# Norms, transposes and stores of a decoder layer's cross stage, one tile at a time

## The chip, the cores and the metric

The kernel runs on one core of a Trainium2 chip. The core has TensorE (PE, with its weight loads PEld), VectorE (DVE), ScalarE (ACT), GpSimd (POOL) and SyncE (SP, which issues the DMAs here). The metric is the device time in microseconds of one execution, median over runs. All data is f32; matmuls in f32r run in one pass and those in f32 in several.

## The reference, cut to what matters

One layer over 8 batches of 512 tokens with 512 features and 16 heads of 32: a causal self-attention with a second linear attention ("memory"), then cross-attention to a context, then two experts with a top-2 gate. Behind each stands a layer norm of the sum with its input.

```python
x = _layernorm(x + _L0_attn_ref(x, ...))
x = _layernorm(x + _L0_xattn_ref(ctx, ctx, x, Wv, Wk, Wq, Wo, bo))   # second norm
x = _layernorm(x + _L0_ffn_ref(x, gate_w, w0, b0, w1, b1))           # third norm

# _L0_xattn_ref: softmax(q k / sqrt(512)) v over 16 heads, then
out @ Wo.T + bo
# _L0_ffn_ref
weights = softmax(tokens @ gate_w); topk_w, topk_idx = top_k(weights, 2)
e0 = silu(x @ w0.T + b0); e1 = silu(x @ w1.T + b1)
out = e0 * fw[:, 0:1] * (fidx[:, 0:1] == 0) + e1 * fw[:, 1:2] * (fidx[:, 1:2] == 1)
```

## The kernel before, in words

Three stages follow each other: self, memory, cross. The change is in the cross stage, which starts in the last rounds of the memory stage. A batch has 4 **tiles** of 128 tokens and 4 **groups** of 4 heads. The stage is written as a line of **slots** n = 0 to 639. Sixteen slots (`SLOTS`) make a group, 64 (`BATCH_SLOTS`) a batch, and `NS` = 512 slots hold all scores. Each engine runs a function of its own over the same slots (`cross_slot_tensor`, `_scalar`, `_vector`, `_gpsimd`, `_sync`) and executes its instructions strictly in that order. Semaphores alone tie the engines. Which slot an instruction stands in is thus its place in its engine's queue. `at` is the slot within the group.

In each slot PE makes one transposed score product (L1353, `bank 2 + n % 2`) and, 22 slots ahead (`CROSS_LEAD`), one product for row maxima (L1325). ACT turns the first into an exp (L1572), DVE takes the maximum of the second (L1335). PE's product of slot n waits for the exp of slot n - 2. Every fourth slot PE multiplies exps and values (L1385). POOL adds the exps of a group in three additions of 128 x 2048 (L1795, at slots 7, 11 and 15 of the group), and PE sums them over partitions at slot 4 of the next group (L1418, "totals"). DVE makes four reciprocals of them (L1643) and y (L1650). At `at` 11 PE transposes the next group's maxima, at 12 ACT copies them (L1547), at 13 DVE subtracts for the low part (L1655) and SP stores both as two rows into the operand stack (`store_shift`, "cross_shift"). The first score product of the next group waits for these.

Batch b's **work behind** its attention runs in the slots of the following batches (`behind(n)` gives the batch and its own slot number, 0 to 127; batch b's slot 0 is n = 64 (b + 1)). All four tiles go through each step together. The output projection and bias are at slots 12 to 27 (L1452, L1432, PE), with the residual addition L1670 and the statistics L138, L140 on DVE tile by tile. POOL computes the factors of all four tiles with four small operations of 128 x 4 at slot 29 (`Norm.factors`, L146 to L152). ACT applies the second norm at slots 31 to 34 (L157). PE transposes at 35 to 38, one chunk of features across all tiles each (L1464), ACT copies the high part x2t_hi (L1587), DVE makes the low part x2t_lo (L1677). The gate is at 39 to 42: 12 matmuls with 8 weight columns and 512 tokens (L163 to L165), whose result is copied and transposed back at 44 (L1592, L1477). DVE picks the top two from 128 x 32 (`cross_gate_first`, `cross_gate_weights`, 15 small operations). The eight units of experts (4 tiles x 2 experts) are at slots 48 to 71 (L1503). Each goes through ACT's tanh (L1601), DVE's silu (L1687), ACT's weighting (L1606) and POOL's addition to x2 (L1775). The third norm has its statistics at 62, 68, 74 and 80, factors of all tiles at 81, applies at 83 to 86, and one store of 1 MB at 87 (L1848).

Batch 7's work has no scores beside it. It runs in slots 512 to 639 by the same functions.

## Time and profile before

| | us |
|---|---|
| median of 3 runs | 1872.0 |
| lowest and highest | 1866.68, 1873.97 |
| profiled execution | 1871.82 |
| its span | 1869.9 |

| engine | busy us | share of the span |
|---|---|---|
| PE | 1743.1 | 93% |
| DVE | 1266.4 | 68% |
| POOL | 1084.1 | 58% |
| ACT | 967.5 | 52% |

The profile is one execution. A line is named by its number in the kernel; a name such as `bank` or `x` is a tile without its buffer number, and a helper's line is shared by all its callers (L157 is every norm's apply). Idle time is put down to what came last before the engine went on.
### The profile page before, as it was taken

The page shows a single profiled execution, that of the slowest core. Times are in us where ns is not written, and L with a number is a line of the kernel's source. Part 1 is how long each engine was busy: PE and PEld are TensorE (multiplying, and loading weights), DVE is VectorE, ACT ScalarE, POOL GpSimd, SP SyncE. Part 2 cuts the span into 40 slices and gives each one's busy share as a digit, 9 for nine tenths or more (in the row PEclk, how much of TensorE's full clock was granted, in tenths as well). Part 3 has the DMA queues.
Part 4 walks back from the last instruction along what each step waited for, and adds up shares of the span by engine and source line. Part 5 has one row for each costly group of instructions (what it writes and reads, how often), then busy time and mean ns, then how long its engine had stood idle before and what let it go on. Part 6 is the DMA issues. An engine that isn't in the chain of part 4 may idle for free.

```text
span 1869.9 us, 29831 instructions
## 1 busy us (share of the span) xinstructions
PE 1743.1 (93%) x10442; PEld 1092.0 (58%) x10442; DVE 1266.4 (68%) x2747; ACT 967.5 (52%) x1893; POOL 1084.1 (58%) x741
## 2 busy tenths in 40 slices
PE   5999999999999889999977999999999999999886
PEld 4666666666666368877733465554645546455444
DVE  5677777777777477778766667667677677676532
ACT  3555555555555423433455555555555555555533
POOL 2555565656554646544577675575665766666552
PEclk9999999999999789999989999999999999999998
DMA  6465655555554545666356334334433344333100
GB/s 195 136 159 152 158 154 151 162 142 166 140 154 123 173 143 164 205 199 192 101 143 145 94 94 119 93 89 119 106 99 97 92 113 119 103 96 102 35 23 23
DMA packets 166496, 237.21 MB, mean 127 GB/s; under 512 B 21318, under 2 KB 72518, under 8 KB 166348
## 3 DMA queue, kind: packets, MB, share of 16 engines
q1 hardware_dynamic: 166348, 235.31, 45.6%
q8 instruction: 84, 1.38, 0.3%
q14 instruction: 64, 0.52, 0.1%
HBM read 91.57 MB, written 41.94 MB: 71 GB/s over the span
## 4 chain that ended last, share of the span: by engine, by line
PE 73%; DVE 7%; POOL 5%; ACT 4%; DMA 4%; issue 3%; SPq 2%; ACTq 0%; POOLq 0%; DVEq 0%
PE bank L1503 9%; PE bank L163 8%; PE bank L164 6%; PE bank L165 6%; PE bank L1452 5%; PE bank L1385 5%; PE bank L313 4%; PE bank L1353 4%; PE bank L258 4%; PE bank L1325 4%; POOL cross_added L1795 4%; PE bank L300 4%; DVE bank L1643 2%; PE bank L278 2%; DVE cross_negmax L1335 2%
## 5 line engine op out<-in xcount | busy, mean ns | idle before, releaser
L1335 DVE TENSOR_REDUCE cross_negmax<-bank 128x1 f32<-128x512 f32 x512 | 342.4, 678 | 213.7 <-PE bank L1325 209.6
L1572 ACT ACTIVATE cpt<-bank 128x512 f32<-128x512 f32 x512 | 299.8, 594 | 216.0 <-PE bank L1353 212.6
L487 DVE CUSTOM_DVE_ANT_0 bank<-bank,future 128x128 f32<-128x128 f32 (+3 forms) x512 | 246.7, 488 | 172.9 <-PE bank L300 172.2
L372 ACT ACTIVATE pt<-bank 128x256 f32<-128x256 f32 (+3 forms) x512 | 224.2, 441 | 256.8 <-PE bank L258 256.0
L1795 POOL TENSOR_TENSOR cross_added<-cross_added,cpt 128x2048 f32<-128x2048 f32 x64 | 292.3, 4566 | 58.1 <-ACT cpt L1572 57.9
L1325 PE MATMUL bank<-cqk 96*128 96x512 f32 x512 | 262.2, 516 | 22.6 <-DMA cqk<-cstage 12.3
L1795 POOL TENSOR_TENSOR cross_added<-cpt,cpt 128x2048 f32<-128x2048 f32 x32 | 146.5, 4577 | 184.9 <-ACT cpt L1572 184.9
L1353 PE MATMUL bank<-cqk 98*128 98x512 f32 x512 | 228.3, 447 | 26.0 <-ACT cpt L1572 18.4
L551 POOL TENSOR_SCALAR_AFFINE_SELECT pt<-pt 128x512 f32<-128x512 f32 x128 | 81.3, 635 | 251.7 <-ACT pt L372 251.6
L163 PE MATMUL bank<-xt_hi,w_hi 128*128 128x512 f32 x384 | 168.9, 440 | 18.8 <-DVE w_lo L445 15.7
L258 PE MATMUL bank<-qk 98*128 98x256 f32 (+2 forms) x512 | 180.1, 355 | 4.2 <-DMA qk<-self_shift 2.5
L1353 PEld LDWEIGHTS bank<-cqk 98*128 98x128 f32 x512 | 98.4, 192 | 146.0 <-ACT cpt L1572 68.1
L300 PE MATMUL bank<-qk 96*128 96x256 f32 (+2 forms) x512 | 165.8, 328 | 4.1 <-DMA qk<-stage 4.1
L164 PE MATMUL bank<-xt_hi,w_lo 128*128 128x512 f32 x384 | 153.5, 400 | 0.0
L165 PE MATMUL bank<-xt_lo,w_hi 128*128 128x512 f32 x384 | 152.3, 397 | 0.0
L1643 DVE RECIPROCAL bank<-bank 128x128 f32<-128x128 f32 x128 | 121.9, 955 | 41.4 <-PE bank L1418 41.4
L1325 PEld LDWEIGHTS bank<-cqk 96*128 96x128 f32 x512 | 99.2, 195 | 79.0 <-DVE cross_negmax L1335 34.0
L1385 PE MATMUL bank<-cpt,cv 128*32 128x512 f32 x1024 | 140.6, 622 | 0.0
L258 PEld LDWEIGHTS bank<-qk 98*128 98x128 f32 x512 | 98.0, 193 | 69.7 <-ACT pt L372 45.1
L1452 PE MATMUL bank<-wo,cy 128*128 128x512 f32 x256 | 134.4, 614 | 0.0
L1775 POOL TENSOR_TENSOR x<-x,tanh 128x512 f32<-128x512 f32 x64 | 82.5, 1289 | 85.4 <-ACT tanh L1606 84.3
L500 DVE RECIPROCAL bank<-bank 128x128 f32<-128x128 f32 x128 | 122.1, 958 | 8.8 <-PE bank L278 8.8
(172 smaller groups left out, 3463.5 us busy)
## 6 DMA issues: line engine op xcount, KB each, us to landing
qk<-stage SPq DMA_DIRECT2D x384, 128.0 KB, 2.3
cqk<-cstage SPq DMA_DIRECT2D x384, 128.0 KB, 2.3
scratch_memory<-memory SPq DMA_DIRECT2D x32, 512.0 KB, 3.8
ma<-scratch_memory SPq DMA_DIRECT2D x32, 512.0 KB, 4.0
raw<-in_x_t SPq DMA_DIRECT2D x32, 256.0 KB, 2.8
v<-in_x SPq DMA_DIRECT2D x32, 256.0 KB, 3.3
scratch_y_ar<-y_ar SPq DMA_DIRECT2D x32, 256.0 KB, 2.2
my_ar<-scratch_y_ar SPq DMA_DIRECT2D x32, 256.0 KB, 4.5
```

The source lines that it names most:

```text
L163: pe.matmul(out, a[0], b[0], start=first, stop=False)
L164: pe.matmul(out, a[1], b[0], start=False, stop=False)
L165: return pe.matmul(out, a[0], b[1], start=False, stop=last)
L258: pe.matmul(bank[:, 0:SEQ - q0], kq[0:98, 1, j, first:first + P], kq[0:98, 0, j, q0:SEQ], start=True, stop=True).then_inc(s.pe_st, 1)
L300: pe.matmul(bank[:, 0:max(keys, 256)], kq[0:96, 0, j, tile_of(qt)], kq[0:96, 1, j, 0:max(keys, 256)], start=True, stop=True).then_inc(s.pe ...
L487: dve.tensor_tensor_reduce(out=scores, in0=scores, in1=sh.future[:, SEQ - P * (qt + 1):SEQ], scale=-1.0, scalar=-NEG, op0=ALU.add, op1=ALU ...
L1325: pe.matmul(max_bank(sh, m)[:, :], kq[0:96, 0, jm, tile_of(qt)], kq[0:96, 1, jm, :], start=True, stop=True).then_inc(s.pe_mx, 1)
L1335: dve.reduce_max(s.negmax[gm % 2][:, col:col + 1], max_bank(sh, m)[:, :], AX, negate=True).then_inc(s.dve_max, 1)
L1353: pe.matmul(sh.bank[2 + n % 2][:, :], kq[0:98, 1, j, tile_of(kt)], kq[0:98, 0, j, :], start=True, stop=True).then_inc(s.pe_st, 1)
L1385: done = pe.matmul(sh.bank[4][rows_of(j), :], s.v[g % 2][:, kt, rows_of(j)], s.pt[step % 3][:, j, :], start=(kt == 0), stop=(kt == TILES - ...
L1572: act.activation(s.pt[step % 3][:, j, :], sh.bank[2 + n % 2][:, :], ACT.Exp, scale=SCALE_CROSS).then_inc(s.act_exp, 1)
L1795: pool.tensor_tensor(s.added[:, :, :], old[:, :, :], s.pt[step % 3][:, :, :], ALU.add).then_inc(s.pool_add, 1)
```

## The change

Both norms of the cross stage get a class of their own, `TileNorm`, which has the statistics, factors and apply of one tile and counts semaphores per tile. In the batches 0 to 6 the second norm's factors stand at slots 18, 22, 26, 30 and its applies at 20, 24, 28, 32. The transposes are by tile (one tile's four chunks of features), at 25, 29, 31, 34, with the copies of the high and low part in the next two slots. The gate and its transposition back stand one slot earlier. The third norm's factors stand at 63, 69, 75, 81, its applies at 65, 71, 77, 83, and each tile has its own store of 256 KB at 66, 72, 78, 84, with two semaphores in turn. The shift rows' subtraction and stores move from `at` 13 to 12, on DVE and on SP.

Batch 7 leaves the slots. These end at 536, and a written-out part follows on each engine (`tail_...`). There three quarters of the projection of tiles 0 and 1 come ahead of the wait for the last group's y. Each tile then has norm, transposes, gate, two experts, third norm and store behind one another; the gate multiplies with the tokens as weights (128 x 128) and the 8 gate columns as data, so that the logits need no transposition. x3, in place of x2, lies in the operand stack that the last groups no longer use.

```diff
+class TileNorm:
+    def __init__(self, nc, sb, sem, name):
+        self.stats, self.mv = sb(f"{name}_stats", [P, TILES, 6]), sb(f"{name}_mv", [P, TILES, 2])
+        self.rstd, self.shift = sb(f"{name}_rstd", [P, TILES]), sb(f"{name}_shift", [P, TILES])
+        self.power = sb(f"{name}_power", [P, TILES])
+        self.vec, self.root, self.applied = sem(f"{name}_vec"), sem(f"{name}_root"), sem(f"{name}_applied")
+    def statistics(self, dve, b, k, r):
+        t = TILES * b + k
+        if b > 0:
+            dve.wait_ge(self.root, 4 * (t - TILES) + 5)
+        dve.bn_stats(self.stats[:, k, :], r).then_inc(self.vec, 1)
+        dve.wait_ge(self.vec, 2 * t + 1)
+        dve.bn_aggr(self.mv[:, k, :], self.stats[:, k, :]).then_inc(self.vec, 1)
+    def factors(self, pool, b, k):
+        t, ks = TILES * b + k, slice(k, k + 1)
+        pool.wait_ge(self.vec, 2 * t + 2)
+        if b > 0:
+            pool.wait_ge(self.applied, t - TILES + 1)
+        pool.tensor_scalar(self.rstd[:, ks], self.mv[:, ks, 1], EPS, None, ALU.add).then_inc(self.root, 1)
+        pool.wait_ge(self.root, 4 * t + 2)
+        pool.tensor_tensor(self.rstd[:, ks], self.rstd[:, ks], self.power[:, ks], ALU.pow).then_inc(self.root, 1)
+        pool.wait_ge(self.root, 4 * t + 3)
+        pool.tensor_tensor(self.shift[:, ks], self.mv[:, ks, 0], self.rstd[:, ks], ALU.mult).then_inc(self.root, 1)
+        pool.wait_ge(self.root, 4 * t + 4)
+        pool.tensor_scalar(self.shift[:, ks], self.shift[:, ks], -1.0, None, ALU.mult).then_inc(self.root, 1)
+    def apply(self, act, b, k, out, r):
+        act.wait_ge(self.root, 4 * (TILES * b + k) + 5)
...
-CROSS_SLOTS = range(SLOTS_BEHIND[LAST + 7][1], NS + 2 * BATCH_SLOTS)
+CROSS_SLOTS = range(SLOTS_BEHIND[LAST + 7][1], NS + 25)
...
+        self.x3 = Place(nc, ATTENTION + LAST_FREE * STACK_BYTES, TOP)("x3", [P, TILES, DIM])
...
+LAST_BATCH = BATCH - 1
 def behind(n):
     b, r = divmod(n, BATCH_SLOTS)
-    return [(bb, r + more) for bb, more in ((b - 1, 0), (b - 2, BATCH_SLOTS)) if 0 <= bb < BATCH]
-PROJECT, APPLY, TRANSPOSE, GATE, LOGITS, EXPERT = 12, 31, 35, 39, 44, 48
-STATS3, FACTORS3, APPLY3, STORE = 62, 81, 83, 87
+    return [(bb, r + more) for bb, more in ((b - 1, 0), (b - 2, BATCH_SLOTS)) if 0 <= bb < LAST_BATCH]
+PROJECT, FACTORS, APPLY, TRANSPOSE = 12, (18, 22, 26, 30), (20, 24, 28, 32), (25, 29, 31, 34)
+GATE, LOGITS, EXPERT = 38, 43, 48
+STATS3, FACTORS3, APPLY3, STORE = (62, 68, 74, 80), (63, 69, 75, 81), (65, 71, 77, 83), (66, 72, 78, 84)
...
+    if slot in TRANSPOSE:
+        k = TRANSPOSE.index(slot)
+        pe.wait_ge(s.ln2.applied, TILES * b + k + 1)
+        if k < 2:
+            pe.wait_ge(s.dve_po, TILES * b + 3 + k)
         else:
-            pe.wait_ge(s.dve_x2t, GROUPS * b + c - 1)
-        for k in range(TILES):
-            done = pe.transpose(sh.bank[6 + c % 2][:, tile_of(k)], s.x2[:, k, tile_of(c)], sh.ident[:, :])
+            pe.wait_ge(s.dve_x2t, TILES * b + k - 1)
+        for c in range(GROUPS):
+            done = pe.transpose(sh.bank[6 + k % 2][:, tile_of(c)], s.x2[:, k, tile_of(c)], sh.ident[:, :])
...
+        pe.wait_ge(s.dve_x2t, TILES * (b + 1))
...
+    if slot in APPLY:
+        k = APPLY.index(slot)
+        if b >= 1:
+            act.wait_ge(s.out_stored[k % 2], 16 * (2 * b - 1 + k // 2))
+        s.ln2.apply(act, b, k, s.x2[:, k, :], s.x1[:, k, :])
+    if slot - 1 in TRANSPOSE:
+        k = TRANSPOSE.index(slot - 1)
         if k == 0 and b >= 1:
-            act.wait_ge(s.out_stored, 16 * b)
-        s.ln2.apply(act, b, k, s.x2[:, k, :], s.x1[:, k, :])
-    if TRANSPOSE + 1 <= slot < TRANSPOSE + 1 + GROUPS:
-        c = slot - TRANSPOSE - 1
-        if c == 0 and b >= 1:
             act.wait_ge(s.pe_ex, UNITS * b)
-        act.wait_ge(s.pe_x2t, GROUPS * b + c + 1)
-        act.activation(s.x2t_hi[:, c, :], sh.bank[6 + c % 2][:, :], ACT.Copy).then_inc(s.act_x2t, 1)
+        x2t_high(act, s, sh.bank[6 + k % 2], b, k)
...
+    if slot in APPLY3:
+        k = APPLY3.index(slot)
...
-    if at == 13 and 0 <= g + 1 < NG:
+    if at == 12 and 0 <= g + 1 < NG:
...
+    if slot - 2 in TRANSPOSE:
+        k = TRANSPOSE.index(slot - 2)
+        x2t_low(dve, s, sh.bank[6 + k % 2], b, k)
...
+    if slot in STATS3:
+        k = STATS3.index(slot)
...
+        if slot in FACTORS:
+            s.ln2.factors(pool, b, FACTORS.index(slot))
...
+        if slot in FACTORS3:
+            s.ln3.factors(pool, b, FACTORS3.index(slot))
...
+def cross_store(sp, s, b, k, x):
+    sp.wait_ge(s.ln3.applied, TILES * b + k + 1)
+    if 2 * b + k // 2 > 0:
+        sp.wait_ge(s.out_stored[k % 2], 16 * (2 * b + k // 2))
+    sp.dma_start(s.t["out"][b, tile_of(k), :], x[:, k, :]).then_inc(s.out_stored[k % 2], 16)
...
-    if at == 13 and 0 <= g + 1 < NG:
+    if at == 12 and 0 <= g + 1 < NG:
...
+        if slot in STORE:
+            cross_store(sp, s, b, STORE.index(slot), s.x2)
...
+def tail_tensor(pe, s, cw, sh):
+    pe.wait_ge(s.act_exp, NS)
+    pe.wait_ge(s.dve_max, NS)
+    for k in (0, 1):
+        tail_project(pe, s, cw, sh, k, range(GROUPS - 1))
+    for k in (0, 1):
+        tail_project(pe, s, cw, sh, k, (GROUPS - 1,))
+    tail_project(pe, s, cw, sh, 2, range(GROUPS))
+    tail_transposed(pe, s, sh, 0)
+    tail_project(pe, s, cw, sh, 3, range(GROUPS))
+    tail_transposed(pe, s, sh, 1)
+    for k in range(TILES):
+        tail_gate(pe, s, cw, sh, k)
+        for i in range(2):
+            tail_expert(pe, s, cw, sh, 2 * k + i)
+        if k + 2 < TILES:
+            tail_transposed(pe, s, sh, k + 2)
...
+def tail_project(pe, s, cw, sh, k, chunks):
+    b = LAST_BATCH
+    for c in chunks:
+        if c == 0:
+            cross_bias(pe, cw, sh.bank[k], 0)
+        pe.wait_ge(s.dve_norm, (TILES + 1) * (GROUPS * b + c + 1))
+        done = pe.matmul(sh.bank[k][:, :], s.y[:, (GROUPS * b + c) % (GROUPS + 1), tile_of(k)], cw.wo[:, c, :],
+                         start=False, stop=(c == GROUPS - 1))
+        if c == GROUPS - 1:
+            done.then_inc(s.pe_po, 1)
...
+def tail_gate(pe, s, cw, sh, k):
+    pe.wait_ge(s.dve_x2t, GROUPS * LAST_BATCH + k + 1)
+    pe.wait_ge(s.dve_po, TILES * LAST_BATCH + k + 1)
+    for c in range(GROUPS):
+        done = triple(pe, sh.bank[k][:, 0:EXPERTS], (s.x2t_hi[:, c, tile_of(k)], s.x2t_lo[:, c, tile_of(k)]),
+                      (cw.gate_hi[:, c, :], cw.gate_lo[:, c, :]), c == 0, c == GROUPS - 1)
+    done.then_inc(s.pe_gate, 1)
...
+def tail_scalar(act, s, sh):
+    b = LAST_BATCH
+    act.wait_ge(s.pe_st, NS)
+    act.wait_ge(s.pe_mx, NS)
+    for k in range(TILES):
+        s.ln2.apply(act, b, k, s.x3[:, k, :], s.x1[:, k, :])
+        if k in (1, 2):
+            if k == 1:
+                act.wait_ge(s.pe_ex, UNITS * LAST_BATCH)
+            x2t_high(act, s, sh.bank[4 + (k - 1) % 2], b, k - 1)
+    for k in range(TILES):
+        act.wait_ge(s.dve_gate, GATE_OPS * (b + k) + GATE_FIRST)
+        act.activation(gate_scratch(sh.bank[k], 1, 1), s.ge[:, k:k + 1, :], ACT.Exp).then_inc(s.act_gate, 1)
+        tail_tanh(act, s, sh, 2 * k)
+        tail_weigh(act, s, 2 * k)
+        tail_tanh(act, s, sh, 2 * k + 1)
+        if k + 2 < TILES:
+            x2t_high(act, s, sh.bank[4 + k % 2], b, k + 2)
+        if k >= 1:
+            s.ln3.apply(act, b, k - 1, s.x3[:, k - 1, :], s.x3[:, k - 1, :])
+        tail_weigh(act, s, 2 * k + 1)
+    s.ln3.apply(act, b, TILES - 1, s.x3[:, TILES - 1, :], s.x3[:, TILES - 1, :])
...
+def x2t_high(act, s, bank, b, k):
+    act.wait_ge(s.pe_x2t, TILES * b + k + 1)
+    act.activation(s.x2t_hi[:, :, tile_of(k)], bank[:, :].rearrange("p (c q) -> p c q", q=P),
+                   ACT.Copy).then_inc(s.act_x2t, 1)
...
+def tail_vector(dve, s, sh):
+    b = LAST_BATCH
+    dve.wait_ge(s.x1_landed, 16 * (b + 1))
+    for k in range(TILES):
+        dve.wait_ge(s.pe_po, TILES * b + k + 1)
+        dve.tensor_tensor(s.x1[:, k, :], sh.bank[k][:, :], s.x1[:, k, :], ALU.add).then_inc(s.dve_po, 1)
+        dve.wait_ge(s.dve_po, TILES * b + k + 1)
+        s.ln2.statistics(dve, b, k, s.x1[:, k, :])
+        if k >= 2:
+            x2t_low(dve, s, sh.bank[4 + k % 2], b, k - 2)
+    for k in range(TILES):
+        dve.wait_ge(s.pe_gate, b + k + 1)
+        cross_gate_first(dve, s, sh.bank[k], b + k, k, 1)
+        cross_gate_weights(dve, s, sh.bank[k], b + k, UNITS * b, k, 1)
+        tail_silu(dve, s, sh, 2 * k)
+        if k >= 1:
+            tail_statistics(dve, s, k - 1)
+        tail_silu(dve, s, sh, 2 * k + 1)
+        if k + 2 < TILES:
+            x2t_low(dve, s, sh.bank[4 + k % 2], b, k + 2)
+    tail_statistics(dve, s, TILES - 1)
...
+def x2t_low(dve, s, bank, b, k):
+    dve.wait_ge(s.act_x2t, TILES * b + k + 1)
+    dve.tensor_tensor(s.x2t_lo[:, :, tile_of(k)], bank[:, :].rearrange("p (c q) -> p c q", q=P),
+                      s.x2t_hi[:, :, tile_of(k)].bitcast(F32), ALU.subtract).then_inc(s.dve_x2t, 1)
...
+def tail_gpsimd(pool, s):
+    b = LAST_BATCH
+    for k in range(TILES):
+        s.ln2.factors(pool, b, k)
+    for u in range(UNITS):
+        x = s.x3[:, u // 2, :]
+        pool.wait_ge(s.act_w, UNITS * b + u + 1)
+        pool.wait_ge(s.pe_x2t, GROUPS * b + u // 2 + 1)
+        if u % 2 == 1:
+            pool.wait_ge(s.pool_x2, UNITS * b + u)
+        pool.tensor_tensor(x, x, s.tanh[u % 2][:, :], ALU.add).then_inc(s.pool_x2, 1)
+        if u >= 2 and u % 2 == 0:
+            s.ln3.factors(pool, b, u // 2 - 1)
+    s.ln3.factors(pool, b, TILES - 1)
```

## Rows read from the trace of the kernel before

**Rows 1.** Windows of two batches: span, busy us (count) PE PEld DVE ACT POOL, clock, DMA

```profile
1173.50:1286.90 113.40, 108.15 (x488) 60.55 (x488) 78.40 (x140) 63.68 (x114) 73.15 (x33) 0.97 0.40 103
1286.90:1398.90 112.00, 106.73 (x488) 59.01 (x488) 78.34 (x140) 63.46 (x114) 73.18 (x33) 0.98 0.40 104
```

**Rows 2.** Waits of PE, 905 to 1800 us: engine line <- releaser: total, times, longest

```profile
PE bank L1353 <- ACT cpt L1572: 18.4, 27, 2.6
...
PE bank L1353 <- DMA cqk<-cross_shift: 7.3, 15, 1.0
PE bank L163 <- DVE x2t_lo L1677: 6.5, 7, 0.9
```

**Rows 3.** Timeline, PE, 1286 to 1312: start, us, operation xcount [idle before <-releaser]

```profile
1286.91 0.50 PE L1353 MATMUL bank<-cqk 98*128 98x512 f32 x1 [0.63 <-DMA cqk<-cross_shift]
...
1289.91 0.50 PE L1353 MATMUL bank<-cqk 98*128 98x512 f32 x1 [0.22 <-ACT cpt L1572]
...
1291.10 0.50 PE L1353 MATMUL bank<-cqk 98*128 98x512 f32 x1 [0.46 <-ACT cpt L1572]
...
1292.77 0.50 PE L1353 MATMUL bank<-cqk 98*128 98x512 f32 x1 [0.95 <-ACT cpt L1572]
...
1296.08 1.04 PE L1418 MATMUL bank<-cross_added,ones 128*32 128x512 f32 x8
...
1298.79 0.66 PE L1464 MATMUL bank<-ident,x 128*128 128x128 f32 x4 [0.33 <-DVE x2t_lo L1677]
...
1300.84 0.39 PE L163 MATMUL bank<-x2t_hi,gate_hi 128*8 128x512 f32 x1 [0.92 <-DVE x2t_lo L1677]
...
1311.68 0.51 PE L1353 MATMUL bank<-cqk 98*128 98x512 f32 x1 [0.31 <-DMA cqk<-cross_shift]
```

**Rows 4.** Timeline, ACT, 1288 to 1289 us

```profile
1288.56 0.81 ACT L157 ACTIVATE x<-cx,ln_shift,ln_rstd 128x512 f32<-128x512 f32 x1 [2.54 <-POOL ln_shift L152]
```

**Rows 5.** Timeline, POOL, 1281 to 1295 us

```profile
1281.85 4.59 POOL L1795 TENSOR_TENSOR cross_added<-cross_added,cpt 128x2048 f32<-128x2048 f32 x1 [2.16 <-ACT cpt L1572]
...
1286.83 1.04 POOL L148 TENSOR_TENSOR ln_rstd<-ln_rstd,ln_power 128x4 f32<-128x4 f32 x1
1287.95 0.20 POOL L150 TENSOR_TENSOR ln_shift<-ln_mv,ln_rstd 128x4 f32<-128x4 f32 x1
...
1288.43 1.26 POOL L1757 TENSOR_TENSOR cstage<-cstage 128x512 fp32r<-128x512 f32 x1
1289.93 4.56 POOL L1795 TENSOR_TENSOR cross_added<-cross_added,cpt 128x2048 f32<-128x2048 f32 x1 [0.23 <-ACT cpt L1572]
```

**Rows 6.** Timeline, PE, 1250 us

```profile
1250.68 0.50 PE L1325 MATMUL bank<-cqk 96*128 96x512 f32 x1 [1.05 <-DVE cross_negmax L1335]
```

**Rows 7.** Windows of 3 us behind stalls: columns as in rows 1

```profile
1180.00:1183.00 3.00, 2.92 (x11) 2.44 (x11) 1.29 (x2) 2.19 (x5) 1.08 (x1) 0.50 0.83 191
1252.00:1255.00 3.00, 3.00 (x9) 1.07 (x11) 0.97 (x3) 1.12 (x2) 2.86 (x3) 0.53 0.02 5
```

**Rows 8.** Timeline, PE, at the last batch's first projection

```profile
1800.24 0.47 PE L1432 MATMUL bank<-bias_rows,bias_ones 128*128 128x512 f32 x1 [1.30 <-DVE cy L1650]
```

**Rows 9.** Chain of waits, 1799 to 1870 us: start, us, engine tile line xcount

```profile
1811.71 3.45 PE bank L1452 x8
...
1818.94 2.94 ACT x L157 x4
...
1821.92 1.13 PE bank L1464 x4
...
1850.15 2.80 PE bank L1503 x12
...
1862.42 0.81 ACT x L157
```

**Rows 10.** DMA issues: out<-in engine op xcount, KB each, us to landing

```profile
x_group<-scratch_x SPq DMA_DIRECT2D x32, 256.0 KB, 2.9
```

**Rows 11.** Groups by line, 905 to 1800: xcount | busy, mean ns | idle

```profile
L1702 DVE TENSOR_REDUCE gate_max<-bank 128x4 f32<-128x32 f32 x7 | 1.2, 169 | 0.0
```

166 lines of the change are left out of this document (96 added, 70 removed).

## The prediction

> **What bounds the kernel now.** I read the stretches first. From 1173 to 1737 us the cross stage repeats itself, one batch of 64 slots in 113.4 or 112.0 us, with PE busy 107 to 108 of it, DVE 78, POOL 73, ACT 63 [rows 1]. So PE sets the pace, the others have room on average, and only what makes PE wait, or adds to its work, can move this stage. The waits of PE come next: by releaser they are ACT's exps (18.4 us), the DMA of the shift rows (7.3) and x2t_lo (6.5) [rows 2]. PE's timeline places them, alike in each of batches 0 to 6. In one batch, slots 32 to 48, they are 0.63 (shift rows, slot 32), 0.22, 0.46 and 0.95 (exps, slots 33 to 35), 0.33 (transpose) and 0.92 (gate) for x2t_lo, and 0.31 (shift rows, slot 48): together 3.82 us [rows 3]. The exps are late because ACT, which works in order, stands 2.54 us before the first of four applies of the second norm, for POOL's factors of all four tiles; POOL makes these at slot 29, behind a 4.6 us addition [rows 4, 5]. A stall of 1.05 us near slot 75 is DVE's: reciprocals, silu and norm statistics stand together there [rows 6]. TensorE's granted clock fell to its lower level of 1.2 GHz (0.53) behind that stall, and in the batch of 113.4 us also behind the exps' stalls (0.50) [rows 7]; the batches that took 112.0 had only the first fall. The difference, 1.4 us, is what I take for one fall. Four of the seven batches had this second fall.
>
> Last comes the chain behind the last scores. It is serial by whole batches: project four tiles, norm, transposes, gate, then eight experts, norm, one store [rows 8, 9].
>
> **The change, part by part.** (1) *Shift rows one slot earlier.* DVE's subtraction goes ahead of one row maximum and one residual addition, some 1.2 us on DVE's queue. SP's two small stores and their landing follow by that much. The stalls of 0.63 and 0.31 are both shorter than 1.2, so both go. What is late next at slot 32 is DVE's maximum of two slots before. DVE waits here for ACT's copy of slot 12, and the maximum of that slot stands behind it; PE has two banks for maxima, so I cost this at 0, and at 0.3 if that cover is gone.
>
> (2) *Factors tile by tile.* POOL's set of four small operations takes 1.9 us for four columns: power 1.04, the next one 0.20, and from the addition's end at 1286.44 to the key residual at 1288.43 all four took 1.99 with gaps, 1.9 without the first [rows 5]. For one column nothing in the trace shows the price. Bounds: 1.94 (no part of it grows with columns) and 1.1 (the power falls to 0.20 like its neighbour). I take 1.5, in the middle. A batch has eight sets for two: 8 x 1.5 - 3.9 = 8 us more on POOL, 81 of some 109 us; 5 and 12 are the ends. POOL has that on average. What counts is the place, since its queue is in order, with 4.6 us additions in it.
>
> The first set of the second norm (slot 18) now stands behind the last of the third (slot 81, which is slot 17 of the next batch), and both behind an addition. ACT may wait up to 1.5 us at slots 19 and 20. PE has the 2 us of weighted sums and totals right there and exps are needed two slots later: 0. The sets at 22 and 26 fall into POOL's gaps between additions: 0. The set at slot 30 starts like today's, behind the addition of slot 27. But ACT waits for it at slot 32 instead of 31, with one apply behind it and not four, and PE has 2.8 us of work of slot 32 to do (1286.91 to 1289.91, less the 0.22) [rows 3]. So the 0.22, 0.46 and 0.95 go.
>
> The new edge is in POOL's queue: addition (4.6), set (1.5), key residual (1.26), addition (4.6) [rows 5]. With PE freed of its waits it reaches the totals (L1418, slot 36), which want that last addition, near 1293.5 on the old clock of the timeline, with the transposes moved ahead counted in. POOL is done at 1282.2 + 4.6 + 1.5 + 1.3 + 4.6 = 1294.2. **A new wait of 0.7 us**; 0.3 with sets of 1.1, 1.2 with sets of 1.94. Today PE comes at 1296.1 [rows 3], behind POOL's 1289.93 + 4.56 = 1294.5.
>
> (3) *Transposes by tile at slots 25, 29, 31 and 34; gate at 38.* The instructions are as many and as large. Each waits for one apply that is 4 or more slots old, except the last (slot 34, apply at 32). The residuals x2t_lo leave the slots in which DVE also has four reciprocals, so the waits of 0.33 and 0.92 go. DVE still has a reciprocal and a maximum in each of slots 37 to 40. The nearest row for what that does to PE is the 1.05 us of [rows 6], where silu and statistics stand there as well; I take 0.3 us of new wait, nearer to nothing since these two are absent, with 0 and 1.05 as ends.
>
> (4) *Third norm and stores by tile.* The applies move from slots 19 to 22 to slots 65, 71, 77 and 83, 0.7 us of ACT each, where PE's exps are one slot ahead or PE is in expert or projection work: 0, at most 0.3 each. The stores are 256 KB on SP, each behind a wait for ACT of the slot before. Behind the store of slot 66 SP's stack load is queued, behind that of 72 the keys. These wait for DVE of the same slot and for landed stacks anyway. The 1.05 us stall stays, since DVE's work there is the same.
>
> A batch thus loses 3.8 us of stalls and gains 0.7 + 0.3: **2.8 us**, times 7 is 19.7. The four falls of the clock behind ACT's stalls go with them: 4 x 1.4 = 5.6; nothing of it, if stalls of 0.7 us bring them too. Here a rule speaks: by the Trainium skill ("TensorE: Matmul & The Clock Gate", Part 4), transposes don't count for the clock gate as matmuls do. By that rule the sparse slots 28 to 37, which now get three of the transposes, may bring a fall in all batches, and this term would be lost or turn to +4. No row read here separates transposes from matmuls in this. The rival below is priced from rows.
>
> (5) *The last batch.* Today PE stands 1.30 us for the last head group's y before it projects at 1800.24 [rows 8]. Now three quarters of tiles 0 and 1 are projected in that time: start 1798.9. From there PE works nearly without a break, since each tile's norm and residuals hide under the next tile's projection (3.7 us; DVE's add and statistics, POOL's set and ACT's apply are on three engines and overlap from tile to tile) or experts. Its stream by [rows 9]: projections 14.9 (1800.2 to 1815.2); four tiles of transposes, 1.13 us each at half clock, so 0.57 at the full one: 2.3; eight experts of 12 matmuls in 2.80 and one for the bias, 3.03: 24.2; four gates. A gate is 12 matmuls with 128 x 128 weights and only 8 columns. Nearest rows: 0.23 for one with 512 columns (2.80 / 12), 0.14 for a transpose with its load (0.57 / 4). That is 12 x 0.14 = 1.7 at most by the nearer one, 2.8 by the other, 0.6 at the least (a column of eight for free, the load at a third); I take 1.5, so 6.0. The sum is 47.4: last expert ends at 1846.3, where today it ends at 1856.0.
>
> Behind the last expert today: 6.45 us through tanh, silu, weight, POOL's addition, statistics and factors to the first apply at 1862.42 (the last expert ends 3.03 after the 1852.95 of [rows 9]). Now ACT's queue has the apply of tile 2 before the last weighting, and that apply waits for POOL: +1.0 (0 to 1.7); the set is shorter by 0.4. One apply (0.73) follows instead of four, and a store of 256 KB, 2.9 us to land by a load of that size [rows 10], where today's 1 MB store is issued at 1862.42 + 4 x 0.73 = 1865.4 and the span ends 4.5 later. So 1846.3 + 7.05 + 0.73 + 2.9 = 1857.0, against a span of 1869.9: **12.9 us** saved; 8 with gates of 2.8, 17 with 0.6. I cost the gate's small DVE operations (0.17 each, 15 a tile, 2.6 us [rows 11]) at nothing: the 3.0 us of the next expert cover them. Without that cover ACT's weighting would be late once, by 1 us.
>
> By the Trainium skill ("GPSIMD Engine Reference", 3.1) an instruction of that engine pays a fixed dispatch and then goes by elements. This case's rows [rows 5] have 0.20 us for four columns of a product and leave open which part of the power's 1.04 is fixed. By the rule taken at its strictest, sets stay at 1.94 and the sum is 3.5 us less gain; with 1.1 it is 3 us more.
>
> The sum: 19.7 + 5.6 + 12.9 = 38.2. The profiled execution took 1871.8 with a span of 1869.9, and the median of the runs is 1872.0, so they are one. 1871.8 - 38.2 = 1833.6, said as **1834**.
>
> **The rivals.** *POOL becomes the bound.* Sets of 1.94 and late starts make PE wait 2.4 us a batch for additions, at the totals and through exps. For it: the queue above is already the last to finish. Against: on average POOL has 25 us of room in a batch. A batch then saves 3.8 - 2.4 - 0.3 = 1.1, 7.7 in all, the clock falls in every batch (3 more, +4.2), the tail saves 12.9 less 0.4: 16, so 1856. *The clock falls as often as now or more, all else as forecast*: 1834 + 5.6 = 1839, or 1844 with three falls more. *All covers hold*: sets of 1.1, no new waits, gates of 0.6: 26.7 + 5.6 + 17 = 49, so 1823. *Slower*: head-of-line waits. POOL's eight sets each wait for DVE's statistics with a 4.6 us addition queued behind, and ACT waits eight times a batch in front of an exp. Today one such wait of 2.54 us costs PE 1.63 [rows 3, 4]. If each set cost PE 1.2 us, a batch is 9.6 - 3.8 = 5.8 longer, times 7 less 12.9 is +28, so 1900. It turns slower than before from 0.71 us a set on: 7 x (8 x 0.71 - 3.8) = 13, the tail's gain. Against it: POOL is idle for 40 us of each batch, and only the sets of slots 30, 63, 75 and 81 stand at an addition. *The change doesn't do what it says in the batches* (stalls move to DVE, which then has 1.05 us or more at two places): 1872 - 12.9 + 0 to 4, so 1859 to 1863.
>
> **How the numbers follow.** Forecast with its own bounds (1828 to 1843, the clock rival in it) 0.55; all covers hold 0.15; POOL the bound 0.17; nothing in the batches 0.08; slower 0.05. The range that holds 8 in 10 is 1820 to 1857. A measurement of this kernel can tell about 0.5% (9.4 us) from no change. Faster by more (under 1862.6): the first three and most of the fourth, 0.9; within it: 0.05; slower by more: 0.05.
>
> **What would show it.** Batches of some 107 to 109 us between the same rows. PE's waits for cross_shift and x2t_lo gone, those of L1353 for exps under 5 us in the stage, a wait of the totals for cross_added of about 0.7 us in each batch (none: sets cheaper than 1.5; 2 us: the rival). One fall of the clock a batch, not two. POOL's power on one column near 0.6 us. In the tail no idle of PE over 0.5 us from projection to last expert, gates of 1.5 us, and 10.7 us from the last expert to the end. What would make it wrong: new waits of DVE's maxima where the residuals now stand (slots 27, 31, 33, 36), and falls of the clock that I can't place.

## The result and the profile after

| | us |
|---|---|
| median before, of 5 runs beside the changed kernel | 1872.0 (1865.65 to 1874.38) |
| median after, of 5 runs | 1817.17 (1814.3 to 1818.78) |
| ratio, 95% interval | 0.9712 (0.969 to 0.9734) |
| forecast | 1834 (1820 to 1857) |
| profiled span after, before | 1815.4, 1869.9 |

The kernel became 54.8 us faster, 2.9%. The direction was right, the gain was forecast as 38.2 us, and the time lies 2.8 us under the range. By the spans the gain is 54.5 us.

The page of the changed kernel: busy time of each engine, and the granted clock in 40 slices. Line numbers are now those of the changed file: L1405 is the score product for the exps, L1376 the one for the maxima, L1470 the totals, L1846 POOL's addition of exps, L195 every norm's apply.

```profile
PE 1729.1 (95%) x10474; PEld 1092.8 (60%) x10474; DVE 1266.5 (70%) x2792; ACT 963.2 (53%) x1895; POOL 1133.6 (62%) x933
...
PEclk9999999999999869999988899999999999999999
```

Two windows of one batch each, and one of 4 us in the second of them (columns as in [rows 1]):

```profile
1178.20:1284.50 106.30, 104.20 (x490) 58.99 (x489) 77.83 (x139) 62.86 (x114) 79.38 (x56) 1.00 0.42 110
1284.50:1392.20 107.70, 105.78 (x491) 59.23 (x489) 77.83 (x139) 63.20 (x114) 79.34 (x56) 0.98 0.41 109
...
1348.00:1352.00 4.00, 3.97 (x14) 1.37 (x13) 2.28 (x6) 1.81 (x5) 3.69 (x5) 0.57 0.04 8
```

A batch takes 106.3 us, where it took 112.0 or 113.4 [rows 1]. Of the six batches behind 1072 us, the one of 107.7 us is the only one in which the granted clock fell (0.57 in four microseconds). By these two windows a fall again costs 1.4 us. Other traces of this kernel and its variants give 1.1 to 1.7 (second trace: 107.50 with a fall, 106.33 without; third norm of tile 2 later: 107.55 and 105.90). POOL is busy 79.4 us of a batch where it was 73.2, so the eight sets for two added 6.2 us. DVE's and ACT's work is the same to 0.6 us.

PE's waits from 850 to 1745 us, to be held against [rows 2]:

```profile
PE bank L1405 <- ACT cpt L1623: 11.0, 15, 2.5
PE bank L1376 <- DMA cqk<-cstage: 9.4, 4, 4.3
PE bank L1376 <- DVE cross_negmax L1386: 9.1, 15, 1.0
PE bank L1470 <- POOL cross_added L1846: 3.0, 7, 0.5
```

The waits for the shift rows (7.3 us) and for x2t_lo (6.5) are gone. Those for exps are down from 18.4 to 11.0, and most of what is left lies ahead of 1040 us, where the stage fills: from 1040 to 1745 they are 3.3 us. New is a wait of the totals for POOL's addition, once in every batch. In the settled part of a batch these stalls of PE are left (timeline, PE):

```profile
1283.44 1.07 PE L1470 MATMUL bank<-cross_added,ones 128*32 128x512 f32 x8 [0.45 <-POOL cross_added L1846]
...
1347.49 0.49 PE L1376 MATMUL bank<-cqk 96*128 96x512 f32 x1 [1.05 <-DVE cross_negmax L1386]
```

With one of 0.20 us and one of 0.07 behind DVE and one of 0.12 behind ACT that makes 1.9 us in the window of 107.7 us, where it was 5.3 in the window of 112.0. A batch without a fall has one more, of 0.16 us behind ACT near slot 79, so 2.1. The stall of 1.05 us is that of [rows 6], unchanged.

POOL's timeline around the set of slot 30, to be held against [rows 5]:

```profile
1271.44 4.57 POOL L1846 TENSOR_TENSOR cross_added<-cross_added,cpt 128x2048 f32<-128x2048 f32 x1 [0.79 <-ACT cpt L1623]
1276.10 0.22 POOL L185 TENSOR_SCALAR ln_rstd<-ln_mv 128x1 f32<-128x1 f32 x1
1276.40 0.57 POOL L187 TENSOR_TENSOR ln_rstd<-ln_rstd,ln_power 128x1 f32<-128x1 f32 x1
1277.04 0.19 POOL L189 TENSOR_TENSOR ln_shift<-ln_mv,ln_rstd 128x1 f32<-128x1 f32 x1
1277.32 0.22 POOL L191 TENSOR_SCALAR ln_shift<-ln_shift 128x1 f32<-128x1 f32 x1
1277.50 1.27 POOL L1808 TENSOR_TENSOR cstage<-cstage 128x512 fp32r<-128x512 f32 x1
1278.73 4.57 POOL L1846 TENSOR_TENSOR cross_added<-cross_added,cpt 128x2048 f32<-128x2048 f32 x1
```

The queue is the one that the forecast wrote down: addition, set, key residual, addition, without a gap, and PE's totals follow its end at 1283.3. The set takes 1.40 us to the key residual's start.

The last batch: a window between batch 6's last expert and the last expert of all, then the timeline of PE (batch 6's last expert matmul, tile 0's transposes and gate, the last expert matmul), and that of ACT and SP at the end:

```profile
1759.10:1804.50 45.40, 45.40 (x204) 32.77 (x202) 25.60 (x96) 19.15 (x32) 19.71 (x41) 1.00 0.08 30
```

```profile
1758.49 0.40 PE L1553 MATMUL bank<-exp_lo,x2t_hi 128*128 128x512 f32 x1
...
1773.83 0.60 PE L1993 MATMUL bank<-ident,x 128*128 128x128 f32 x4
1774.19 0.25 PE L201 MATMUL bank<-gate_hi,x2t_hi 128*128 128x8 f32 x1
1774.30 0.25 PE L202 MATMUL bank<-gate_hi,x2t_lo 128*128 128x8 f32 x1
...
1775.53 0.48 PE L1484 MATMUL bank<-bias_rows,bias_ones 128*128 128x512 f32 x1
...
1804.37 0.40 PE L2015 MATMUL bank<-exp_lo,x2t_hi 128*128 128x512 f32 x1
```

```profile
1806.81 0.81 ACT L195 ACTIVATE x<-x,ln_shift,ln_rstd 128x512 f32<-128x512 f32 x1 [1.42 <-POOL ln_shift L191]
1807.53 0.71 ACT L2062 ACTIVATE tanh<-tanh,gate_w 128x512 f32<-128x512 f32 x1
1812.09 0.81 ACT L195 ACTIVATE x<-x,ln_shift,ln_rstd 128x512 f32<-128x512 f32 x1 [3.85 <-POOL ln_shift L191]
...
1812.93 0.33 SPq L1863 DMA_DIRECT2D out<-x  x1
```

PE is busy 45.40 of 45.40 us at the full clock. From the last expert of batch 6 to the end of the span it took 71.0 us before (1800.24 less the idle 1.30 [rows 8], so 1798.94, to 1869.9) and takes 56.5 now (1758.89 to 1815.4): 14.5 us less.

### The profile page after: what moved, and what is told of

The parts are those of the page before. It is cut to its first block, busy times and chain, and to the rows that moved or that the text cites. A ratio compares the mean times of both kernels' runs of the same rounds, so it can differ in the third digit from the quotient of the medians.

```text
span 1815.4 us, 30316 instructions
## 1 busy us (share of the span) xinstructions
PE 1729.1 (95%) x10474; PEld 1092.8 (60%) x10474; DVE 1266.5 (70%) x2792; ACT 963.2 (53%) x1895; POOL 1133.6 (62%) x933
## 4 chain that ended last, share of the span: by engine, by line
PE 69%; POOL 9%; DVE 8%; DMA 4%; issue 4%; ACT 3%; SPq 3%; POOLq 0%; ACTq 0%; DVEq 0%
PE bank L201 8%; PE bank L1553 8%; PE bank L202 6%; PE bank L203 6%; POOL cross_added L1846 5%; PE bank L351 5%; PE bank L296 4%; PE bank L1376 4%; PE bank L1437 4%; PE bank L1405 4%; PE bank L338 4%; PE bank L1504 2%; SPq L684 2%; DVE cross_negmax L1386 2%; PE bank L316 2%
## 5 line engine op out<-in xcount | busy, mean ns | idle before, releaser
L1623 ACT ACTIVATE cpt<-bank 128x512 f32<-128x512 f32 x512 | 295.9, 595 | 160.9 <-PE bank L1405 153.9
L1846 POOL TENSOR_TENSOR cross_added<-cross_added,cpt 128x2048 f32<-128x2048 f32 x64 | 292.3, 4567 | 27.4 <-ACT cpt L1623 26.7
L1376 PE MATMUL bank<-cqk 96*128 96x512 f32 x512 | 254.9, 501 | 20.4 <-DMA cqk<-cstage 9.4
L1405 PE MATMUL bank<-cqk 98*128 98x512 f32 x512 | 227.7, 445 | 12.0 <-ACT cpt L1623 11.0
L1846 POOL TENSOR_TENSOR cross_added<-cpt,cpt 128x2048 f32<-128x2048 f32 x32 | 146.5, 4577 | 107.0 <-ACT cpt L1623 107.0
L1405 PEld LDWEIGHTS bank<-cqk 98*128 98x128 f32 x512 | 98.1, 192 | 123.5 <-ACT cpt L1623 54.8
L1376 PEld LDWEIGHTS bank<-cqk 96*128 96x128 f32 x512 | 98.0, 193 | 76.6 <-DVE cross_negmax L1386 31.7
L201 PEld LDWEIGHTS bank<-xt_hi,w_hi 128*128 128x128 f32 x384 | 73.9, 193 | 88.4 <-issue 73.8
L603 POOL TENSOR_TENSOR self_added<-self_added,pt 128x1024 f32<-128x1024 f32 x64 | 117.6, 1838 | 5.3
```

The source lines that it names most:

```text
L201: pe.matmul(out, a[0], b[0], start=first, stop=False)
L1376: pe.matmul(max_bank(sh, m)[:, :], kq[0:96, 0, jm, tile_of(qt)], kq[0:96, 1, jm, :], start=True, stop=True).then_inc(s.pe_mx, 1)
L1405: pe.matmul(sh.bank[2 + n % 2][:, :], kq[0:98, 1, j, tile_of(kt)], kq[0:98, 0, j, :], start=True, stop=True).then_inc(s.pe_st, 1)
L1623: act.activation(s.pt[step % 3][:, j, :], sh.bank[2 + n % 2][:, :], ACT.Exp, scale=SCALE_CROSS).then_inc(s.act_exp, 1)
L1846: pool.tensor_tensor(s.added[:, :, :], old[:, :, :], s.pt[step % 3][:, :, :], ALU.add).then_inc(s.pool_add, 1)
```

## The experiments

The theory under test was that of the forecast, in parts: each stall has a place in a queue, and an edit that changes the place removes it. The rival for the whole was that the waits only move on. For the clock there were two theories: a fall follows a stall of about 1 us (the stall theory), or it depends on the place in time as well, so that the length of a batch decides how many stalls bring one (the place theory). The letters A and B in the expectations are each run's own. All stalls below are of settled batches, 1040 to 1790 us.

**Shift rows alone.** The kernel before, with the rows one slot earlier on DVE and SP:

```diff
-    if at == 13 and 0 <= g + 1 < NG:
+    if at == 12 and 0 <= g + 1 < NG:
```

> The kernel before with one part of the change: the shift rows' subtraction on DVE and their stores on SP at slot 12 of the group instead of 13. By the forecast's step 1 the two stalls of 0.63 and 0.31 us a batch behind cross_shift go, 0.94 x 7 = 6.6 us, with the granted clock falling as often as before: 1865. Rival (theory B, the clock): the stalls' lengths matter less than how often the clock falls; a batch that is 0.9 us shorter moves the 1.05 us stall of slot 75 against whatever the clock gate goes by, and the number of falls changes, each worth 1.4 us: between 1865 - 14 = 1851 and 1870.

Measured: 1873.45 us, ratio 1.0008 (0.9991 to 1.0026), above both the theory (1865) and its rival (up to 1870). The waits for the rows went, from 7.0 to 0.4 us, but those for exps grew from 12.1 to 16.5. Its waits of PE, and the stall that took their place:

```profile
PE bank L1353 <- ACT cpt L1572: 16.5, 20, 2.0
...
PE bank L1353 <- DMA cqk<-cross_shift: 0.4, 1, 0.4
```

```profile
1291.45 0.50 PE L1353 MATMUL bank<-cqk 98*128 98x512 f32 x1 [0.97 <-ACT cpt L1572]
```

This was 0.22 us [rows 3]. ACT comes to that exp late because of POOL's factors, whenever PE arrives. Over the five batches from one 1.05 us stall to the sixth (1139.62 to 1702.70, before 1137.25 to 1701.31) the gain is 1.0 us; ten falls of the clock lie in that stretch, eight before, which took back 2.8. So the edit alone is worth 0.76 us a batch of PE's time, nearly the 0.94 forecast, and the clock takes it back. The trace shows that the falls came; why they came here, it doesn't.

**Shift rows back, in the changed kernel** (the same two lines the other way).

> The changed kernel with the shift rows back at slot 13 on DVE and SP. With the transposes moved to slots 25 to 34, PE reaches the group's first product later, so the DMA's stall is smaller than the 0.63 us before. Theory A (rows are worth what they were): 0.3 to 0.6 us a batch back, 2 to 4 us: 1820. Rival: another batch length makes the clock fall more often, up to one more in each of 6 batches at 1.4 us: up to 1829.

Measured: 1835.31 us, ratio 0.981 (0.9775 to 0.9844), 18 us slower than the changed kernel, and more than the theory (1820) or its rival (1829) had. PE waits 14.1 us for the rows, nearly all of it at slot 48, up to 2.93 us:

```profile
1410.88 0.80 PE L1405 MATMUL bank<-cqk 98*128 98x512 f32 x1 [2.93 <-DMA cqk<-cross_shift]
```

DVE's timeline says what stands ahead of the subtraction (L1706): the first nine operations of the gate, which the change put one slot earlier, at slot 44.

```profile
1404.69 0.18 DVE L1752 TENSOR_REDUCE gate_max<-bank 128x4 f32<-128x32 f32 x1
...
1405.73 0.16 DVE L1769 TENSOR_SCALAR gate_keep<-bank 128x4 f32<-128x4 f32 x1
1405.81 0.68 DVE L1386 TENSOR_REDUCE cross_negmax<-bank 128x1 f32<-128x512 f32 x1
1406.40 0.27 DVE L1706 TENSOR_TENSOR cross_shift<-bank,cross_shift 16x128 fp32r<-16x128 f32 x1
```

So the same edit is worth nothing on the kernel before and 18 us on the changed one. It is part of the gate's move.

**Transposes and gate at their old slots**, in the changed kernel, still by tile:

```diff
-PROJECT, FACTORS, APPLY, TRANSPOSE = 12, (18, 22, 26, 30), (20, 24, 28, 32), (25, 29, 31, 34)
-GATE, LOGITS, EXPERT = 38, 43, 48
+PROJECT, FACTORS, APPLY, TRANSPOSE = 12, (18, 22, 26, 30), (20, 24, 28, 32), (35, 36, 37, 38)
+GATE, LOGITS, EXPERT = 39, 44, 48
...
-    if slot - 2 in TRANSPOSE:
-        k = TRANSPOSE.index(slot - 2)
+    if slot - 1 in TRANSPOSE:
+        k = TRANSPOSE.index(slot - 1)
```

> The changed kernel with the transposes back in slots 35 to 38 and the gate back in 39 to 42 (logits 44), but still tile by tile behind factors and applies by tile; x2t_lo is made in the slot behind each transpose, as before. What is left of the change is factors, applies, third norm, shift rows and the tail. Theory A (the 0.33 and 0.92 us that PE waited for x2t_lo are due to where the transposes and residuals stand): both are back, 1.2 us a batch, 8 to 9 us in seven batches, and since DVE's gate operations stand a slot later ahead of the shift rows' subtraction nothing is gained there: 1825 to 1827 us, the waits of the exps not back. Theory B (those waits were a result of ACT's late applies, and the factors by tile alone remove them): within 3 us of the changed kernel's 1817, and the only wait is the totals' one, shorter than 0.45 us or gone because PE comes four transposes... later to everything but the totals.

Measured: 1857.92 us, ratio 0.9926 (0.9903 to 0.995), 41 us slower than the changed kernel. Both theories missed the size. PE's waits for x2t_lo are 23.3 us (20.4 at the gate, 2.9 at the transposes), and the granted clock falls in each of the six batches, in five of them for about twice as long as elsewhere (0.82, 0.50 and 0.82 in the three windows of 4 us from 1298 to 1310). PE's wait at the gate was 0.92 us [rows 3] and is now 2.92:

```profile
1298.02 0.63 PE L1515 MATMUL bank<-ident,x 128*128 128x128 f32 x4 [0.42 <-DVE x2t_lo L2090]
...
1302.02 0.59 PE L201 MATMUL bank<-x2t_hi,gate_hi 128*8 128x512 f32 x1 [2.92 <-DVE x2t_lo L2090]
```

DVE's timeline in the same place:

```profile
1298.38 0.96 DVE L1694 RECIPROCAL bank<-bank 128x128 f32<-128x128 f32 x1
1299.25 0.67 DVE L2090 TENSOR_TENSOR x2t_lo<-bank,x2t_hi 128x512 fp32r<-128x512 f32 x1
1299.84 0.68 DVE L1386 TENSOR_REDUCE cross_negmax<-bank 128x1 f32<-128x512 f32 x1
1300.43 0.96 DVE L1694 RECIPROCAL bank<-bank 128x128 f32<-128x128 f32 x1
1301.30 0.67 DVE L2090 TENSOR_TENSOR x2t_lo<-bank,x2t_hi 128x512 fp32r<-128x512 f32 x1
```

The first product of the gate is for all four tiles. When PE transposed by chunks of features, it waited for three of the four residuals (in the kernel before, `pe.wait_ge(s.dve_x2t, GROUPS * b + max(c + 1, 3))`). By tile it waits for the fourth, which comes 2.05 us after the third (1299.25, 1301.30), behind a maximum and a reciprocal. So by tile the transposes must be early: the two edits are one.

**Batch 7 left in the slots**, all else as changed (the `tail_...` parts are not called, and the slots run to the end):

```diff
-CROSS_SLOTS = range(SLOTS_BEHIND[LAST + 7][1], NS + 25)
+CROSS_SLOTS = range(SLOTS_BEHIND[LAST + 7][1], NS + 2 * BATCH_SLOTS)
```

> The changed kernel, with batch 7 left in the slots (512 to 639) by the same functions as the other batches, and no written-out tail. It prices the tail. Theory (the tail is worth what the two traces show behind the last expert of batch 6: 71.0 us before, 56.3 after): slower than the changed kernel by 10 to 15 us, since norm and stores by tile in the slots hide a part: 1829 to 1832, ratio to before 0.978. Rival: the tiles' norms in the slots already give most of the tail's gain, the written-out part under 5 us: 1821.

Measured: 1826.35 us, ratio 0.9758 (0.9732 to 0.9784), 9.2 us slower than the changed kernel, between the theory (1829 to 1832) and its rival (1821). From batch 6's last expert (1763.5) to the end of the span (1826.1) it is 62.6 us: 8.4 less than before by the norms' new places alone, and another 6.1 by the part written out. The rest of the 9.2 is in the batches, where this trace has four falls of the clock and the changed kernel's one. At the end PE still waits:

```profile
PE bank L1514 <- ACT x L195: 2.2, 1, 2.2
PE bank L201 <- DVE x2t_lo L2084: 1.4, 1, 1.4
PE bank L1483 <- DVE cy L1698: 1.3, 1, 1.3
```

**How thin the covers are.** The changed kernel with one more power of one column in each set, 0.65 us a set:

```diff
+        pool.tensor_tensor(self.spare[:, ks], self.rstd[:, ks], self.power[:, ks], ALU.pow).then_inc(self.root, 1)
+        pool.wait_ge(self.root, 5 * t + 4)
```

> The changed kernel with one more power of one column (result unused) in every set of factors: +0.65 us on POOL for each of 64 sets. Forecast's step 2: only the set of slot 30 stands in the queue that PE's totals wait for, so the wait of L1470 grows from 0.45 to 1.1 us a batch, 4.5 us in 7 batches, and 0.65 to 2.6 us in the tail: 1823. Rival (POOL or ACT head-of-line at several sets): 0.65 at two or more sets a batch, 9 us and more plus falls of the clock: 1830 or above.

Measured: 1833.17 us, ratio 0.9785 (0.9749 to 0.9821), 16 us slower. Stalls of 0.78, 0.81 and 0.55 us for exps came up in the batches without a fall (108.4 us), of which the first is behind the set of slot 30 and the others behind the third norm's sets. The totals' wait stayed as it was:

```profile
1284.36 0.50 PE L1407 MATMUL bank<-cqk 98*128 98x512 f32 x1 [0.78 <-ACT cpt L1625]
1288.34 1.06 PE L1472 MATMUL bank<-cross_added,ones 128*32 128x512 f32 x8 [0.45 <-POOL cross_added L1848]
```

So with sets 0.65 us longer the head-of-line rival begins to come true, at three of the eight sets, 2.1 us a batch, and the sets of 1.4 us fit with less than that to spare.

**The 1.05 us stall, first attempt.** The row maximum of slot 9 of a group ahead of y and silu on DVE:

```diff
+    if SLOT_MAX <= m < NS and at == 9:
+        cross_max_taken(dve, s, sh, m)
...
-    if SLOT_MAX <= m < NS:
+    if SLOT_MAX <= m < NS and at != 9:
```

> The changed kernel with DVE's row maximum ahead of y and of the batch's silu in slot 9 of a group (slot 73 of a batch). If the 1.05 us stall of slot 75 is the maximum standing behind y and silu (0.6 each) on DVE, it shrinks to 0 to 0.4 us in six batches, 4 to 6 us, and the falls behind it go: 1811. Rival: DVE is behind by its sum of work since slot 69, and PE then waits at another maximum or for y: 1816 to 1818.

Measured: 1843.48 us, ratio 0.9855 (0.9819 to 0.9891), 26 us slower; a miss. The 1.05 went, and PE's waits for exps rose to 19.0 us, with stalls of 1.47 us one slot behind the old place, 1.13 near slot 98, and single ones up to 2.3. Behind the first of these stands ACT's weighting (L1656), which has exps behind it and now waits 1.62 us for silu, where it waits 1.02 in the changed kernel. What makes the stall near slot 98 isn't shown.

```profile
PE bank L1405 <- ACT cpt L1623: 19.0, 14, 2.3
```

```profile
1134.85 0.72 ACT L1656 ACTIVATE tanh<-tanh,gate_w 128x512 f32<-128x512 f32 x1 [1.62 <-DVE tanh L1740]
```

**The 1.05 us stall, second attempt.** The third norm of tile 2 three slots later:

```diff
-STATS3, FACTORS3, APPLY3, STORE = (62, 68, 74, 80), (63, 69, 75, 81), (65, 71, 77, 83), (66, 72, 78, 84)
+STATS3, FACTORS3, APPLY3, STORE = (62, 68, 77, 80), (63, 69, 78, 81), (65, 71, 80, 83), (66, 72, 81, 84)
```

> The changed kernel with the third norm's tile 2 three slots later: statistics from slot 74 to 77, factors from 75 to 78, apply from 77 to 80, store from 78 to 81; nothing else is moved. DVE's two statistics operations (0.68 and 0.18 us) then no longer stand ahead of the row maximum for which PE stands 1.05 us in every batch. Theory A (that stall is DVE's queue at slots 73 to 75, and POOL's and ACT's queues have room for the same work three slots on): the stall shrinks by 0.7 to 0.85, with the 0.1 us of restart 0.8 to 0.9 a batch, and the low place of the clock behind it goes too: 6 to 8 us faster than the changed kernel's 1817, 1809 to 1811. Theory B (what was found when the row maximum was put ahead of y and silu: this order is full on every engine, and work moved out of one queue turns up as a wait for ACT's exps or POOL's addition): the stall shrinks but waits for exps or totals of as much or more appear between slots 78 and 100, 1817 to 1830.

Measured: 1813.32 us, ratio 0.9684 (0.964 to 0.9728). The stall is still 1.05 us in every batch (1241.81, 1347.71, 1453.61 and so on), so this run's theory A was wrong on its cause. DVE's timeline of the changed kernel shows why: the maximum for which PE waits ends at 1347.4, and the statistics come behind it. Ahead of it are a reciprocal, y and silu.

```profile
1345.56 0.67 DVE L1701 TENSOR_TENSOR cy<-bank,cross_y_raw 128x512 f32<-128x512 f32 x1
1346.15 0.68 DVE L1737 SCALAR_TENSOR_TENSOR tanh<-tanh,bank 128x512 f32<-128x512 f32 x1
1346.75 0.68 DVE L1386 TENSOR_REDUCE cross_negmax<-bank 128x1 f32<-128x512 f32 x1
1347.35 0.68 DVE L176 BATCH_NORM_STATS2 ln_stats<-x 128x6 f32<-128x512 f32 x1
```

A batch takes 105.9 us instead of 106.3, the 0.16 us wait for an exp behind slot 78 being gone. It is the fastest kernel of the study, but its interval overlaps the changed kernel's, so that it is faster than that one is not shown.

**The clock.** Five runs bear on it. Two were unchanged kernels, before and after, traced again. Two had one bias matmul of no use added to each expert unit (1.9 us of PE's work a batch) in the kernel before and in the changed one; the fifth had three added to the changed one (5.6 us). In the changed kernel the edit reaches the batches 0 to 6 alone, since the last batch has a function of its own (the expectation of the run with one matmul more says otherwise).

```diff
+        pe.matmul(bank[:, :], cw.row_ones[:, :], cw.rows[:, 1 + i, :], start=True, stop=True)
         cross_bias(pe, cw, bank, 1 + i)
```

> The kernel before, unchanged, once more, to see whether the falls of TensorE's granted clock repeat from one execution to the next. In the first trace there were ten falls in batches 0 to 6, one behind each of the six 1.05 us stalls of slot 75 and four behind ACT's stalls, about 1.4 us each. Theory A (a stall of that length brings a fall): again behind every 1.05 us stall. Theory B (it depends on the stall's place in time against something that runs on its own): another number or another set, within 3 of ten since the batches' lengths are the same.

> The changed kernel unchanged, for a second trace of it. Theory A (the low places of TensorE's granted clock depend only on the program and come at the same times in every execution, as the two traces of the kernel before showed): again one single low place in the seven batches, near 1350 us, and the same span within 2 us. Theory B (how many come is chance, and the first trace of the changed kernel was a lucky one): several low places, at other times, each making the span 1.4 us longer.

> The kernel before with one more bias matmul ahead of each expert unit: 8 x 0.23 = 1.9 us of dense TensorE work in each of 7 batches, 13 us in all, stalls as they were. Theory A: ten to twelve falls as before, 13 us slower, 1886. Theory B: batches of 112.7 + 1.9 us lie otherwise, the number of falls is under eight, and the kernel is slower by 13 less up to 10 us: 1876 to 1883.

> The changed kernel with one more bias matmul, of no use, in each of the eight expert units of a batch, also in the last batch: 1.9 us more of PE's work in a batch, none of it in the slots where PE stalls. It is what was done to the kernel before in the run with a slower PE, where the low places of the granted clock fell from ten to four and 15 us of added work cost 9. Theory A (a low place comes behind a stall of 1 us only at some places in time, so the length of a batch sets how many of the six stalls are hit): the number differs from the changed kernel's one, 0 to 5 at other times, and the time is 1817 + 15 + 1.4 for each further one, 1832 to 1838. Theory B (the changed kernel has few because its stalls are fewer and further apart, whatever the length of a batch): one or none again, 1832.

> The changed kernel with three more bias matmuls (overwritten by the real one) ahead of each expert unit: 24 x 0.23 = 5.6 us of dense TensorE work in each of 7 batches, which brings a batch from 106.3 to about the 112 us it had before, with all stalls left as they are. Theory A (falls of the clock go with the stalls of PE): as in the changed kernel, 1 to 3 falls; 39 us slower than it, 1856. Theory B (whether the 1.05 us stall of slot 75 brings a fall depends on the batch's length): falls behind most of the six 1.05 us stalls again, 39 + 5 x 1.4 = 46 us slower, 1863.

Measured: before again 1871.47 us, span 1869.5; after again 1818.38, span 1816.6; before with one 1881.44, ratio 1.006 (1.0038 to 1.0081); after with one 1833.51, ratio 0.9794 (0.9767 to 0.9822); after with three 1853.02, ratio 0.9899 (0.9846 to 0.9953).

In all traces but one (row maximum first, where it is 1.47 us one slot on) the 1.05 us stall comes six times between 1130 and 1710 us. I looked through windows of 4 us from 1130 to 1790 for a granted clock under 0.97. A low stretch of about twice the usual length counts once; there are five with the transposes late, two with the shift rows back, two with the row maximum first, and one each in rows alone and in before with one matmul more.

| kernel | batch without a fall, us | falls behind the six 1.05 us stalls | elsewhere |
|---|---|---|---|
| before | 110.6 (112.0 less 1.4) | 6 | 4 |
| before, again | 110.6 (112.0 less 1.4) | 6 | 4, same places |
| rows alone | - | 6 | 6 |
| before, one matmul more | 112.2 | 1 | 2 |
| after | 106.3 | 1 (1348) | 0 |
| after, again | 106.3 | 1 (1242) | 0 |
| batch 7 in the slots | 106.3 | 2 | 2 |
| shift rows back | - | 3 | 4 |
| third norm of tile 2 later | 105.9 | 1 | 0 |
| after, one matmul more | 108.2 | 4 | 0 |
| after, three more | 111.8 | 3 | 1 |
| longer sets | 108.4 | 2 | 1 |
| transposes late | - | 0 | 6, at the 2.92 us stall |
| row maximum first | - | 6 (its stalls of 1.47 us) | 2 |

Two windows of the kernel before with one matmul more, the first behind a 1.05 us stall, the second behind a stall of 0.93 us for an exp:

```profile
1142.00:1146.00 4.00, 3.86 (x17) 1.70 (x18) 2.90 (x7) 2.44 (x6) 3.86 (x4) 1.00 0.00 0
1520.00:1524.00 4.00, 4.00 (x16) 2.65 (x19) 1.89 (x3) 2.23 (x5) 1.10 (x1) 0.50 0.84 193
```

The same stalls, to 0.03 us, come with ten falls in the traces of one program and with three in the trace of another that differs only in 1.9 us of matmuls away from them. That is against the stall theory. The 15 us of added work cost 8 by the times (1881.44 against 1873.24 beside it). But whether program or execution made the difference isn't shown: the eight executions with one matmul more lie in two groups, five from 1877.99 to 1882.14 us (the traced one among them) and three from 1887.21 to 1888.86, and those of the kernel before from 1862.46 to 1879.40. The longer group has the lower mean granted clock (0.964 or 0.965 against 0.969 to 0.971). The two executions with three matmuls more are 11 us apart (1847.37, and the traced 1858.67); what makes that, no trace shows. The place theory fits that the number changes, but not that it can be told from the length: 108.2 gives 4, 108.4 gives 2, 112.2 gives 1. And the two traces of the changed kernel have the one fall at different stalls, while those of the kernel before agree in all ten places from 1130 us on. The Trainium skill ("TensorE: Matmul & The Clock Gate", Part 1) says that the unit behind the clock runs freely against the kernel, so that the places vary from run to run. The changed kernel's two traces agree with that (1348 against 1242). Those of the kernel before agree with it ahead of 1030 us, where the stage fills (from 1004 to 1008 us the granted clock is 1.00 in one and 0.65 in the other), and not from 1130 on, with the same ten. What decides which stall is hit stays open.

One more regularity is in the record. The batches of rows alone take 112.6 us each, those of transposes late 112.5 to 112.8 (both have falls in every batch), and those of the kernel before 112.7 in the mean of a pair (113.4 and 112.0), though PE's idle time in them is 4.9, 5.4 and 5.2 us. In rows alone the falls took back most of what the shorter stalls had gained. Why the batches come to the same length isn't shown.

## Where the forecast held, and which steps of it failed

By the trace the gain of 54.5 us is made of 41.4 in the slots of batches 0 to 6 (the last expert of batch 6 ended at 1798.94 and ends at 1758.89, though the stage was 1.35 us later at 920 us), less that 1.35, and 14.5 in the last batch. Forecast were 25.3 (19.7 and 5.6) and 12.9. Of the 16.3 us that were missing in the forecast, 7.0 are the clock (at 1.4 us a fall), 9.1 the stalls, 1.6 the tail, less the 1.35. Two steps failed: the link from stalls to the clock, which was wrong in kind, and the size of the stalls' term. Either alone would have left the time in the range.

**The clock is the step whose mechanism failed**, in the sum behind part 4: four falls of ten were to go and one behind each 1.05 us stall to stay, 5.6 us. Nine went, 12.6 us. The price of one was right (1.4 us by 107.70 less 106.30, 1.1 to 1.7 over all traces). What failed was the link from stall to fall: "behind that stall" was read as "because of that stall", since all six had one. A stall of the same length in the same place came with a fall in 0 to 6 of 6 cases, as the table shows. The rivals reckoned with more falls only, none with fewer. Without these 7.0 us the time would have been 1824. The record doesn't show why the changed kernel's two traces have one fall each and some of its variants' three or four, so a part of the 7.0 us may be luck.

**Stalls, parts 1 to 3: the mechanism was right, the size was not.** Compare two batches with one fall each, of 112.00 us [rows 1] and of 107.70. PE's idle time went from 5.27 to 1.92 us, and its busy time from 106.73 to 105.78. The forecast had 2.8 us for both together, measured are 4.3 (4.1 in the mean of the seven batches: 41.4 less 12.6). Two batches without any fall give the same, from the kernel before and the changed one, both with one matmul more in each expert unit: 112.25 less 108.18 is 4.1, of which 0.92 is busy time.

```profile
1254.35:1366.60 112.25, 107.01 (x497) 60.32 (x497) 78.37 (x140) 63.52 (x115) 73.20 (x33) 1.00 0.39 104
```

```profile
1463.10:1571.28 108.18, 106.09 (x496) 60.37 (x497) 77.83 (x140) 62.79 (x115) 79.31 (x57) 1.00 0.41 108
```

- Of the idle time 3.35 went. All seven stalls that were named went, and with them two that weren't counted, 0.20 us for ACT's apply and 0.16 for a maximum at slot 31. The totals' wait is 0.45 and not 0.7, as the set takes 1.40 and not 1.5 us and the rest of the queue went as written. The 0.3 us that I gave DVE's reciprocals and maxima at slots 37 to 40 didn't come. Waits of 0.20 and 0.07 us for maxima at slots 46 and 36 and of 0.12 for an exp did, and 0.16 for another in batches without a fall.
- The busy time is 0.95 us less, with the same matmuls. In both traces a product behind a stall is shown with 0.50 us, one in an unbroken row with 0.40 and a start every 0.23. Behind a stall the next product starts after 0.33 us (1347.49, 1347.82). Nine stalls went and four came, so by this pair each cost PE some 0.2 us more than its idle column says (0.95 by five); rows alone, with three stalls fewer, had 0.5 us less of busy time (107.7 for 108.2, two falls in each), so 0.16. The starts alone show 0.10 of it. That the rest belongs to the stalls too is a reading; the forecast put all of it at nothing.

**The price of one column**, part 2, was the middle of 1.1 and 1.94, said as 1.5; it is 1.40, with the power at 0.57 us where four columns took 1.04. If the time is a fixed part and one by columns, that makes 0.41 us fixed and 0.16 for a column. The rule of the Trainium skill ("GPSIMD Engine Reference", 3.1) of a dispatch and a part by elements agrees with these two sizes, and its strictest reading, that a set stays at 1.94, is refuted. That "eight sets add 8 us to POOL" was 6.2.

**Transposes**, part 3: the rule of the Trainium skill cited in the forecast ("TensorE: Matmul & The Clock Gate", Part 4), that transposes don't count for the clock as matmuls do, might have brought falls in slots 25 to 37. In the changed kernel's two traces none is there from 1130 us on. It is not seen at work in this kernel.

What the forecast had as separate edits, each with a price of its own, turned out to hang together. The rows' step was priced at 0.94 us a batch; it is 0.76 alone, and 18 us in all when it is missing from the changed kernel. The transposes' place was priced at 1.25 us a batch, and without it the kernel is 41 us slower. The text said what the gate's new slot does for PE and not what its small DVE operations, moved ahead of the subtraction, would do to the shift rows. The sum was of use all the same because the change has all of these edits in it.

**Third norm and stores**, part 4: 0.16 us a batch for an exp near slot 79, by the run with tile 2's norm later, where nothing was forecast and 0.3 an apply was the most. No wait for the stores is among PE's, and the stores of 256 KB land in 2.0 us in the median. But the run with longer sets shows that this cover is under 0.65 us at two of these sets.

**The tail**, part 5: 14.5 us for 12.9. From end to end PE's stream is 45.9 us (1758.89 to 1804.77) and was forecast as 47.4. By the starts of its groups a gate takes 1.34 us (1774.19 to 1775.53), not 1.5, and all four 5.3 for 6.0; a tile's transposes take 0.36 (1773.83 to 1774.19) where half of the chain's 1.13 was taken, 1.4 for 2.3. Projections (14.7 for 14.9) and experts (24.5 for 24.2) came as forecast. From the last expert to the end it is 10.6 us, forecast 10.7, with two misses that cancel: the apply of tile 2 stands ahead of the last weighting for POOL (1806.81, then 1807.53), which costs 1.4 us and not 1.0, and the last store is shorter than the load it was priced by (2.5 us from its issue to the end of the span, against 2.9).

Of the rivals, "all covers hold" (1823) was the nearest in number, but not by its terms: a set took 1.40 us and not 1.1, a gate 1.34 and not 0.6, and there was a new wait. "POOL the bound" and "slower" didn't come: POOL costs PE 0.45 us a batch. The run with longer sets, 16 us slower, shows how soon waits of their kind begin.

## What to carry to other kernels

Where every engine's queue is full, edits to the order don't have prices of their own: ask of each one which of the others it needs, and forecast them together. A stall costs more than its idle column says, here 0.1 to 0.2 us. And that a fall of the clock stands behind a stall in every batch doesn't show that it will be there once the batch has another length: give it a range from none to one for each such stall.

## What the runs showed of the hardware

- TensorE's granted clock fell to its lower level ten times in both traces of one program, and three times in the one trace of a program with the same stalls and 1.9 us more of work in a batch. A fall costs 1.1 to 1.7 us. Work of 15 us added to PE, its bound, made the kernel 8 us slower in the median of eight executions.
- The product behind a stall is followed after 0.33 us, one in an unbroken row after 0.23.
- Matmuls with 128 x 128 weights and 8 columns start every 0.11 us (1774.19, 1774.30), half of the 0.23 for 512 columns that [rows 9] give.
- POOL's power on 128 x 1 takes 0.57 us, on 128 x 4 1.04.
